# The last stage of a decoder block: four gathered rows per unit and one per addition, in place of six per unit

## The reference

```python
y = jnp.einsum('etd,te->td', expert_out, combine)      # 4 of 16 experts for each token, weighted
z = jax.nn.silu(xt @ Ws1.T) * (xt @ Ws3.T) @ Ws2.T     # shared expert, hidden width 2 x 352
return (y + z).reshape(B, S, D)                        # and x = x + this
```

## Time and profile before

| | |
|---|---|
| Time, median of 3 runs | 1992.2 us (1991.07 to 1993.84) |
| Profiled execution, its own time | 1993.37 us |
| Profiled execution, span (first to last instruction) | 1991.8 us |
| Mean granted clock of TensorE | 0.88 |
| Busy, share of the span: PE, DVE, ACT, POOL | 75%, 53%, 35%, 29% |
| First gather of the last stage begins | 1860.77 us |
| Last addition to the residual begins | 1986.30 us |

### The profile page before, as it was taken

The page is one execution under the profiler, slowest core; times in us unless marked ns, Lnnn a source line. Parts: engine busy times, 40 slices in busy tenths (PEclk is TensorE's granted clock), DMA queues, the critical chain, the costliest instruction groups (busy, mean ns, idle before and its releaser), DMA issues. The chain is left out here.

```text
span 1991.8 us, 28978 instructions
## 1 busy us (share of the span) xinstructions
PE 1502.9 (75%) x9512; PEld 687.2 (35%) x9521; DVE 1059.7 (53%) x1809; ACT 694.4 (35%) x1187; POOL 575.4 (29%) x464
## 2 busy tenths in 40 slices
PE   2778787875266667768677774885699999999957
PEld 1344444442011111112111111532366566666423
DVE  6343434346387777876776726851143333333564
ACT  4322221212116766666766683511011111111211
POOL 3000000002534554554544332467200000000462
PEclk9989898987558989898898886787799999999978
DMA  4252516160423555545644451035555645654564
GB/s 169 72 172 61 182 48 195 36 207 31 116 53 96 159 167 147 174 125 147 181 123 135 154 160 70 1 134 204 182 179 179 176 138 176 181 177 137 140 178 131
DMA packets 212442, 273.45 MB, mean 137 GB/s; under 512 B 91984, under 2 KB 159120, under 8 KB 210064
## 3 DMA queue, kind: packets, MB, share of 16 engines
q1 hardware_dynamic: 188880, 181.68, 32.2%
q0 software_dynamic: 12832, 71.44, 10.3%
q10 hardware_dynamic: 10656, 19.40, 2.6%
HBM read 132.29 MB, written 120.06 MB: 127 GB/s over the span
## 5 line engine op out<-in xcount | busy, mean ns | idle before, releaser
L805 DVE TENSOR_REDUCE ca_mx<-ca_sc 128x1 f32<-128x512 f32 x512 | 331.9, 678 | 165.9 <-PE ca_sc L725 163.6
L77 PE MATMUL re_ab<-re_w,re_xt 128*128 x1800 | 297.6, 316 | 42.5 <-DMA re_w<-we_pairs 38.5
L938 ACT ACTIVATE ca_pt<-ca_st 128x512 f32<-128x512 f32 x512 | 274.9, 590 | 37.5 <-PE ca_st L737 37.1
L737 PE MATMUL ca_st<-ca_qs,ca_ks 49*128 49x512 f16 x512 | 110.2, 426 | 155.6 <-ACT ca_pt L938 155.5
L77 PEld LDWEIGHTS re_ab<-re_w,re_xt 128*128 128x128 f16 x1800 | 174.1, 99 | 141.2 <-issue 44.4
L1003 POOL TENSOR_TENSOR ca_wpair<-ca_wraw,ca_wpair 128x704 f16<-128x704 f32 (+1 forms) x96 | 149.3, 1561 | 65.7 <-ACT ca_wpair L895 65.7
L750 PE MATMUL ca_pv<-ca_pt,ca_va 128*32 128x512 f32 x1024 | 163.1, 701 | 0.9 <-DVE ca_turned L818 0.6
L77 PE MATMUL re_yp<-re_w,re_ht 128*128 (+1 forms) x666 | 156.0, 379 | 0.0
L737 PEld LDWEIGHTS ca_st<-ca_qs,ca_ks 49*128 49x128 f16 x512 | 25.3, 94 | 349.6 <-ACT ca_pt L938 287.6
L725 PE MATMUL ca_sc<-ca_ks,ca_qs 48*128 48x512 f16 x512 | 113.1, 438 | 39.5 <-DVE ca_mx L805 20.6
L478 POOL TENSOR_TENSOR sa_yt<-sa_yf,sa_yt 128x512 f16<-128x512 f32 x16 | 18.5, 1156 | 385.0 <-ACT sa_yt L461 385.0
(11 more groups left out here) (235 smaller groups left out, 2415.9 us busy)
## 6 DMA issues: line engine op xcount, KB each, us to landing
re_w<-we_pairs POOLq DMA_DIRECT2D x16, 2176.0 KB, 9.2
ca_wraw<-in_we SPq DMA_DIRECT2D x64, 352.0 KB, 3.8
we_pairs<-ca_wpair SPq DMA_DIRECT2D x64, 352.0 KB, 2.9
slot_rows<-sa_zeros SPq DMA_DIRECT2D x12, 1792.0 KB, 16.0
slot_outs<-re_ys ACTq DMA_DIRECT2D x74, 256.0 KB, 2.0
ca_wraw<-in_we SPq DMA_DIRECT2D x32, 384.0 KB, 4.8
we_pairs<-ca_wpair SPq DMA_DIRECT2D x32, 384.0 KB, 2.9
sa_scratch<-sa_qk SPq DMA_DIRECT2D x16, 512.0 KB, 4.5
```

Of the source, the lines that this page charges most:

```text
L77: last = nc.tensor.matmul(out, lhs(a, c), rhs(b, c), start=(c == 0 and n == 0), stop=(c == chunks - 1 and n == len(PRODUCTS) - 1))
L737: nc.tensor.matmul(st[:, (2 * n + a) % RING, :], ks[rows, b % SLOTS, pair, kt * P:(kt + 1) * P], qs[rows, b % SLOTS, pair, :], start=True, ...
L805: nc.vector.reduce_max(mx[:, qd // 4, qd % 4, 2 * a + jj:2 * a + jj + 1], sc[:, (2 * n + a) % RING, :], AX.X).then_inc(maxed, 1)
L938: nc.scalar.activation(pt[:, (4 * qd + k) % 8, :], st[:, (2 * n + a) % RING, :], ACT.Exp, scale=SCALE).then_inc(exp_done, 1)
```

## The change

The two `combine(3)` of a unit become `combine(2)`, and each addition of a shared tile is followed by `combine(1)`. A unit then takes four rows in place of six, and an addition takes one. The 12 units take 48 rows and the 16 additions 16, which makes the same 64; `combine(len(order))` at the end finds nothing left in either kernel.

```diff
--- before.py
+++ after.py
@@ -1635,14 +1635,15 @@
 
                 for n in range(g * IC, min(g * IC + IC, shared.HIDDEN)):
                     shared.product(dve, nc.vector, n)
-                    combine(3)
+                    combine(2)
                     shared.low_part(dve, nc.vector, n)
-                    combine(3)
+                    combine(2)
                 if g >= 1:
                     for t in range(4 * g - 4, 4 * g):
                         dve.wait_ge(used, len(fetches) - len(order))
                         shared.add(dve, x_sb, t)
                         dve.wait_ge(shared.added, shared.tiles + t + 1)
+                        combine(1)
             combine(len(order))
 
         @block.sync
```

## The result

| | before | after |
|---|---|---|
| Median | 1991.63 us (6 runs, 1989.04 to 1995.36) | 1972.58 us (6 runs, 1964.30 to 1974.55) |
| Ratio of the two | | 0.9898, 95% interval 0.9877 to 0.9918 |
| Profiled execution, span | 1991.8 us | 1973.0 us |
| Last stage, first up product to last down product | 126.1 us | 105.9 us |

The account below looks back on a forecast made before the run. Additions queued behind early rows hold TensorE in the last stage. Removing 32.1 us and adding 7.56 holes, 5.1 clock and 0.8 tail saves 18.6: from the median 1992.2 to 1973.5 us, range 1966.5 to 1979.

Parts of the forecast that it names:

- What bounds the kernel: Last stage: TensorE sets the end, held 19.74 and 7.31 us by additions queued on VectorE behind rows asked for early.
- Holes: Last stage, TensorE: holes of 27.05 us go; three shorter ones come, 2.64 + 2.46 + 2.46 = 7.56 us.
- Clock: Behind the three new TensorE holes the granted clock falls each time, 1.7 us each, 5.1 in all, ends 0 and 8.4.
- Tail: End of the kernel: row 63's multiply-add follows the last addition and delays the last store by 0.8 us.
- What was called hidden: Single multiply-adds after additions, 0.78 us each, lie beside TensorE's 1.9 us per tile; uncovered, 16 would cost 12.5 us.
- The sum: Whole kernel: 32.1 removed, less 7.56 holes, 5.1 clock and 0.8 tail, saves 18.6 us.
- The clock holds: Rival, last stage: the clock stays up behind all holes or all but one, 1968.4 to 1970.1 us; chance 0.20.
- Rows late: Rival, last stage: gathers slow beside multiply-adds, so the first addition waits for row 23; 1976 to 1980 us; chance 0.15.
- No change: Rival, last stage: the gather stream ends as late as TensorE, needing 1.93 us per gather against 1.38; chance 0.03.
- slower: Rival, last stage: single rows drain the ring, each addition waits for a row, about 4 us each, 2037 us; chance 0.02.
- The "60" rows: Last stage, VectorE: 60 rows were said to stand ahead of the second round's first addition before the change.
- one expectation: For six rows per unit plus one per addition: the second round's hole of 7.3 us would shrink to 4.5.

Follow-up runs that it names:

- one part alone: Changed kernel with four rows per unit but none with the additions: 1988.69 us, 0.9989 of the kernel before.
- the kernel with six rows per unit: Kernel before, six rows per unit kept, with one row added behind each addition: 1992.16 us, 1.0007 of the kernel before.
- holes of 4.04: Changed kernel with 2, 4 and 6 rows in a round's three units instead of 4, 4, 4: 1981.57 us, 0.9954 of the kernel before.
- the single one of 3.07: Changed kernel with each round's last unit cleared of rows, 20/37/56 rows ahead of the additions of tiles 0, 4, 8: 1967.16 us.
- the last expectation: Expected 1965 us for the kernel with last units cleared and 54 rows, not 56, ahead of the third round's first addition; measured 1962.01 us.

## Why the prediction was right

**What bounds the kernel.** Right. TensorE was held in two places by additions that stood behind too many rows; one part alone gave the three holes of 2.46 and left no other.

**Holes.** Predicted 2.64 + 2.46 + 2.46 = 7.56; measured 7.38. The 0.18 is the first hole: I let row 23 limit it, since VectorE had been waiting for just that row. In the run the slow head put the down pair 32.7 us behind the first up product, where it was 31.1, so the gathers had 1.65 us more ahead of it, and VectorE waited for no row. Whether row 23 would have bound in an execution with a fast head was not measured.

**Clock.** Right in kind, off in size. I took three falls at 1.7, 5.1 us; this execution has two falls, 1.49 (5.54 - 4.05) and 1.42 (13.27 - 11.85), 2.9. In its place the head lost 1.65, which is none of the change's doing: the idle time there is the same 3.36 in both, and the kernel with six rows per unit, whose order is the old one up to there, has the slow head too (32.93). Of eleven traces only that of the kernel before has a fast one. The clock is the term of the sum that was mis-sized, by 2.2; the head and the stage's start, 0.7 later, make up 2.3 the other way. That the total came within 0.2 us on these two executions is luck. The page "TensorE: Matmul & The Clock Gate" of the Trainium skill, section "HAM oscillation — how this bites in real kernels", has every wait paid for with a slow start, in a kernel whose waits are about 3 to 5 us. The forecast took it over to holes of 2.46, which are shorter than those, and there it does not hold each time. In all three traces of the changed kernel, and in the one with twelve buffers, the clock held behind the first hole and fell behind the other two of the same length; behind holes of 4.04 all three fell, and behind the single one of 3.07 it held. Nor is it the place: in the kernel without rows at the additions the same three holes of 2.46 cost 1.41, 1.39 and nothing (pairs of 5.46 and 5.44, and 11.85 for the three). What decides stays open; length alone does not. One execution of six took 1964.30, 8 below the median; I have no trace of it.

**Tail.** Predicted 0.8, measured 0.7 (6.23 against 5.50).

**What was called hidden.** Right. The single rows lie beside the down products (1.95 a tile), and leaving them out cost 15.5 at the end. The early stores cost nothing that shows.

**The sum**, against the two profiled executions: holes 27.05 to 7.38, -19.7; clock behind holes 5.05 to 2.9, -2.1; head +1.65; tail +0.7; stage start +0.7. Together -18.8, which is 1991.8 to 1973.0.

**The rivals.** *The clock holds*: no, it fell twice. With matmuls in the holes it held, and the stage, 103.0 less the 1.6 that its slow head lost, is 101.4, where this rival has 126.1 - 32.1 + 7.56 = 101.6. *Rows late*: no wait for a row, and twelve buffers change nothing. Its premise half came true: single gathers took up to 1.90 where 1.35 was the longest before:

```profile
L1608 POOL DMA_INDIRECT co_yg<-slot_outs,fx_index x64: 952/1114/1903, 1861.4 to 1956.8; - x64
...
DMA to landing us min/median/max: 3.4/3.7/5.9
```

The median gather, though, is 1.11 against 1.10, and 24 of them begin within 32.2 us (1861.44 to 1893.67), 1.40 each against 1.37. The Trainium skill's "SBUF — State Buffer", section "Who interferes with whom", has a VectorE instruction with two inputs in SBUF contend with a GpSimd instruction that reads SBUF. It also reports that `tensor_tensor` did not stall transfers issued by GpSimd, so it does not settle what a gather beside a multiply-add does. The trace does in part: the 19 gathers that lie beside no multiply-add, eight of them beside a product or an addition, took 0.95 to 1.03, and all 42 that took 1.07 or more lie beside one. No run here took the multiply-adds away to show the cause. It was too little to matter at eight rows of reserve. *No change* and *slower*: the ring never ran dry; GpSimd waited for VectorE 13 times, 3.7 us at the longest, and VectorE never for GpSimd.

**The slip.** The "60" rows ahead of the second round's addition are 54. It touched no number of the sum, but it turned the sign of one expectation. The 25, 42 and 61 of the last expectation are a slip of the same kind.

## What to carry to other kernels

Where an in-order engine both feeds the critical engine and does deferrable work, count how many deferrable items stand ahead of each release, and set that number by what has arrived by then; then look at the items inside the final chain before the release, because once supply no longer binds, each of those costs its full length (0.78 us of multiply-add became 0.79 of hole, plus clock). Deferred work must not collect at the end: put it beside the critical engine's last stretch, one item per release. Price a hole with the clock's fall behind it, as a chance and not as a certainty, and write out the counts at each release point before arguing from them.

## What the runs showed of the hardware

A TensorE hole of 2.46 us in otherwise dense matmuls cost 1.4 to 1.6 us more through the clock in ten cases and nothing in five, over five traces; the one of 3.07 us cost nothing, and those of 4.04 us cost 1.70 to 2.91 more, three out of three. With nine additional matmuls inside each hole of 2.46 us the clock stayed at 1.00 behind all three. The same 3.36 us of idle time before the stage (3.35 to 3.37) kept the clock at 1.00 in one trace of eleven; in the other ten the clock stood at 0.50 to 0.56 behind it, which cost 1.57 to 1.69 us in nine and 2.82 in one. That is a part of the scatter of single runs and nothing that a kernel's change should be credited with.
